# A graph kernel on one core: the first key's walk begins two steps later beside the second key's scatters

## The reference

```python
ex1 = e * x[src]
ex2 = e * x[dst]
mi = jnp.zeros_like(x).at[dst].add(ex1)
mo = jnp.zeros_like(x).at[src].add(ex2)
h = jnp.concatenate([mi, mo, x], axis=1)
h = jnp.tanh(h @ W1 + b1)
h = jnp.tanh(h @ W2 + b2)
h = jnp.tanh(h @ W3 + b3)
return jnp.tanh(h @ W4 + b4)
```

```python
edge_index = jnp.stack([src, dst])
x = _layernorm(x + _L0_gnn_ref(x, edge_weight1, edge_index, ...), axis=-1)
x = _layernorm(x + _L1_gnn_ref(x, edge_weight, edge_attr_3, edge_index, ...), axis=-1)
```

## Time and profile before

| | us |
|---|---|
| median of three runs | 2017.97 |
| lowest and highest | 2016.92, 2019.26 |
| the profiled execution | 2020.07 |
| its span in the profile | 2018.3 |
| last scatter of the second key begins | 1073.55 |

### The profile page before, as it was taken

One profiled execution on the slowest core, in us unless ns is written; L12 is line 12 of the kernel. 1 busy time (PEld: TensorE's weight loads), 2 busy tenths in 40 slices (PEclk: granted clock), 3 DMA queues, 4 the chain that ended last, 5 costly groups with the idle time before them and its releaser, 6 DMA issues. The chain is left out here.

```text
span 2018.3 us, 22733 instructions
## 1 busy us (share of the span) xinstructions
PE 1246.5 (62%) x5510; PEld 865.2 (43%) x5510; DVE 1086.3 (54%) x3123; ACT 627.4 (31%) x1638; POOL 1254.0 (62%) x1315
## 2 busy tenths in 40 slices
PE   5733444222226754433314689999589999998663
PEld 1311122111114543333203556666357777777553
DVE  9844544333313334544313647777547777776576
ACT  0100000000002210000006956666344444442785
POOL 6477777777757777777773113333488877871244
PEclk8766665666669986665557989999779999999676
DMA  1011111111137864544215535455313333332586
GB/s 34 21 34 33 31 31 34 34 34 34 34 102 213 216 189 131 149 130 136 81 40 134 151 103 155 151 160 154 103 37 79 99 100 84 94 100 79 147 214 167
DMA packets 330291, 204.52 MB, mean 101 GB/s; under 512 B 32299, under 2 KB 318704, under 8 KB 330160
## 3 DMA queue, kind: packets, MB, share of 16 engines
q1 hardware_dynamic: 269008, 140.38, 26.2%
q0 software_dynamic: 35280, 49.84, 8.7%
q10 hardware_dynamic: 25872, 12.85, 2.2%
HBM read 124.03 MB, written 78.92 MB: 101 GB/s over the span
## 5 line engine op out<-in xcount | busy, mean ns | idle before, releaser
L472 POOL DMA_INDIRECT placed<-pay,pos_i x392 | 396.3, 1011 | 155.0 <-issue 135.0
L467 POOL DMA_INDIRECT gat<-in_x,key_i x392 | 395.1, 1008 | 126.8 <-issue 116.3
L1018 DVE TENSOR_TENSOR pay<-bank,wj 128x512 f32<-128x512 f32 x98 | 67.5, 689 | 446.4 <-PE bank L785 432.2
L780 PE MATMUL bank<-ident,gat 128*128 128x128 f32 x98 | 38.8, 396 | 409.8 <-DMA gat<-in_x,key_i 398.3
L514 POOL DMA_INDIRECT gat<-x_d,src_i x196 | 253.2, 1292 | 59.0 <-issue 52.0
L1100 DVE TENSOR_TENSOR res<-res,bank 128x128 f32 x588 | 168.5, 286 | 146.1 <-PE bank L827 34.2
L897 PE MATMUL bank<-prod,ident 128*128 128x280 f32 x896 | 218.3, 402 | 0.0
L827 PE MATMUL bank<-woh,pw 128*128 128x128 f32 x784 | 143.4, 349 | 110.5 <-ACT woh L629 59.2
L780 PEld LDWEIGHTS bank<-ident,gat 128*128 128x128 f32 x98 | 17.6, 180 | 431.4 <-DMA gat<-in_x,key_i 414.4
L55 ACT ACTIVATE xt<-bank 128x128 f32<-128x128 f32 x98 | 26.8, 274 | 549.4 <-PE bank L780 549.3
L897 PEld LDWEIGHTS bank<-prod,ident 128*128 128x128 f32 x896 | 171.8, 192 | 47.0 <-issue 0.6
(11 more groups left out here) (155 smaller groups left out, 2325.9 us busy)
## 6 DMA issues: line engine op xcount, KB each, us to landing
pw<-placed SPq DMA_DIRECT2D x588, 68.0 KB, 2.1
pw<-placed SPq DMA_DIRECT2D x98, 272.0 KB
xin<-in_x_t SPq DMA_DIRECT2D x98, 256.0 KB, 3.1
hot_d<-woh SPq DMA_DIRECT2D x49, 256.0 KB, 2.4
x_d<-res POOLq DMA_DIRECT2D x49, 256.0 KB, 3.8
oh<-hot_d SPq DMA_DIRECT2D x28, 448.0 KB, 4.2
placed<-pay SPq DMA_DIRECT2D x28, 448.0 KB, 5.5
out<-out ACTq DMA_DIRECT2D x49, 256.0 KB, 2.7
```

Of the source, the lines that this page charges most:

```text
L467: pool.indirect_dma_start(gat[:, t, :], None, x, bass.IndirectOffsetOnAxis(ap=key_i[:, 1 - c, t:t + 1], axis=0)).then_inc(s_gat[n // CHUNK ...
L472: pool.indirect_dma_start(placed[c].rearrange("t p r -> (t p) r"), bass.IndirectOffsetOnAxis(ap=pos_i[:, c, t:t + 1], axis=0), pay[i % 4][ ...
```

## The change

The first walk gets a start step: batches 0 to 2 belong to step 2 and not to step 0, and so on, and its last batch to step 18 instead of 16. The second walk begins at step 19 instead of 17, and its last group is in step 43 instead of 41. Nothing is added or taken away.

```diff
-        FIRSTS, LAST_FIRST, EXTRAS = 3, 17, 2
+        FIRSTS, FIRST_FROM, LAST_FIRST, EXTRAS = 3, 2, 19, 2
...
-            return range(min(FIRSTS * q, NG), min(FIRSTS * (q + 1), NG))
+            return range(min(FIRSTS * max(q - FIRST_FROM, 0), NG), min(FIRSTS * max(q + 1 - FIRST_FROM, 0), NG))
```

## The result

| | before | changed |
|---|---|---|
| median, us | 2017.45 (4 runs) | 2003.48 (4 runs) |
| lowest and highest | 2016.83, 2019.26 | 2000.88, 2004.72 |
| span of the profiled execution | 2018.3 | 2002.8 |

The ratio is 0.9928, 95% interval 0.991 to 0.9945: the change makes the kernel faster, by 14.0 us between the medians, 0.55% to 0.9%. The forecast was 2003.0.

What follows compares the result with a forecast made beforehand. POOL's row of DMAs was taken to bound the second key's stage. The profiled 2020.07 us less 15.0 is 2005.1; being 2.1 above the median, the median goes from 2017.97 to about 2003.0, range 2001.0 to 2006.0.

Steps and rivals of the forecast that it cites:

- POOL bounds the stage, and what follows hangs on its last scatter: Second key's steps: each microsecond taken from POOL's row of DMAs moves everything behind it by a microsecond.
- The long wait is for a payload behind three batches: Ahead of group 49's first scatter: POOL loses 14.99 us to a payload whose projection stands behind three walk batches.
- Two steps suffice, with 5.7 us of slack: Change of key: group 51's payload is ready at 597.62, wanted at 603.3; one step would leave POOL starved.
- The overlap costs POOL about 0.1 us: From 582.6 to 597.6, walk loads beside POOL's DMAs: POOL loses 0.05 us on each of two groups.
- The walks' later end costs nothing: Second walk's end: two more loaded steps cost 9.4 us at most, within group 95's 10.3 us lead.
- Rival 1: Between groups 50 and 51: POOL starves if the first walk step grows over 5.7 us; 2010.6 if doubled; chance 5%.
- Rival 2: Change of key: DVE's one-hots in five newly overlapping batches hold POOL 4.4 us, giving 2007.4; chance 4%.
- Rival 3: Ahead of group 49: POOL waits for its queue or positions, not the payload; time stays 2018.0; chance 4%.
- Rival 4: Near the stage's end: the second walk's two steps come out there, 5.7 us slower, 2023.7; chance 2%.
- PE's clock: Behind the stage: 3.6 us at the lower clock, worth about 1.8 us, may fall out or come twice.

Runs made afterwards that it cites:

- experiment 1: Changed kernel with the walks begun one step later than before instead of two; 2007.07 us, ratio 0.9953 to the kernel before.
- experiment 3: Changed kernel with SP's first-walk loads also waiting until group 49's scatters have landed, one group later; 2009.73 us, ratio 0.9964 to the kernel before.
- experiment 10: Changed kernel with four batches of the first walk in a step instead of three; 2019.57 us, ratio 1.0015 to the kernel before.
- experiment 2: Changed kernel with the walks begun three steps later than before instead of two; 2003.58 us, ratio 0.9933 to the kernel before.
- experiment 9: Changed kernel with the second walk four more steps later (steps 23 to 47); 2001.60 us, ratio 0.9923 to the kernel before.
- experiment 11: Changed kernel with four more DVE compares behind each batch of the first walk; 2002.62 us, ratio 0.9922 to the kernel before.
- experiment 4: The changed kernel itself, unaltered, against the kernel before; 2000.90 us, ratio 0.992.
- experiment 8: The changed kernel once more, unaltered, against the kernel before; 2000.93 us, ratio 0.992.
- experiment 5: Changed kernel with the second walk four more steps later (steps 23 to 47), on the slower chip; 2147.01 us, ratio 1.0004 to the kernel before.
- experiment 7: Changed kernel with four more DVE compares behind each first-walk batch, on the slower chip; 2149.47 us, ratio 1.0014 to the kernel before.
- experiment 6: Changed kernel with four first-walk batches in a step instead of three, on the slower chip; 2157.95 us, ratio 1.0058 to the kernel before.

## Why the prediction was right, point by point

- **POOL bounds the stage, and what follows hangs on its last scatter.** Shown: the wait that went was 15.0 us, and in the four comparisons of the changed kernel with the kernel before the medians fell by 14.0, 16.8, 15.7 and 14.5 us. In the first pair of profiles the time behind the last scatter changed by only 0.5 us, but one pair can't show that closely: it is 940.7 to 946.8 us in the four profiles of the changed kernel. Experiments 1, 3 and 10 show the other sign: gaps of 5.9, 7.3 and 19.0 us cost 6.2, 8.8 and 18.6 us.
- **The long wait is for a payload behind three batches.** Shown by experiment 1, which moved it to the next group.
- **Two steps suffice, with 5.7 us of slack.** The size was a little off. Measured, the third payload was ready for POOL 5.0 us early (5.86 less the handover of 0.83). The walk's first step, from the first load to the projection behind it, took 597.47 - 583.61 = 13.9 us instead of 13.3 with POOL's DMAs beside it; I had allowed 2.1 us for that and it cost 0.6; the landing of `xin` in that stretch went from 2.7 us to 3.1, where I had taken 3.4. The next payload came 9.8 us later, and the lead grew to 23 us by group 67. By the prediction's 9.64 us a step it would have come to about 17 (16 steps of 0.7 behind 5.9): the direction was right and the pace was taken from the first step alone, where SP's loads give 9.0. That one step would leave POOL starved was in the prediction too, and experiment 1 has it: 5.9 us.
- **The overlap costs POOL about 0.1 us.** Groups 49 and 50 took (604.45 - 583.86) / 2 = 10.30 us each, less than the 10.33 that I took. Nothing was lost there.
- **The walks' later end costs nothing.** Shown by experiments 2 and 9. The thinnest lead near the end, that of group 95, is 10.3 us before and after, and 10.0 in experiment 9.
- **Rival 1** (third payload late) did not happen, though experiment 3 shows that it was the nearest: its price beyond 5.0 us is one for one, and a single late load in the next step added 1.8 us. On the chip of the slower kind it did come about (last section). **Rivals 2, 3 and 4** are refuted by experiments 11, 1 and 9, on the other chips.
- **The range.** That the forecast came within 0.5 us is in part luck: the gains of the four comparisons lie 2.8 us apart, and the medians of experiments 4 and 8, 2000.90 and 2000.93, are just below the 2001.0 at which the range ends, beside kernels before of 2017.66 and 2016.64. Two parts move between executions of the same kernel: the start of the stage (the second key's first scatter lay at 583.86, 581.27, 579.26 and 580.95 in four profiles of the changed kernel) and the time behind its last scatter (944.3, 940.7, 945.1 and 946.8). The range had a term for PE's clock in the second; how much of it is the clock was not worked out.

## What to carry to other kernels

When an engine sits idle with "issue" as its releaser and nothing else is busy, look at the program order of the engines that feed it: here a wait for the producer's own last transfer had been written ahead of the next piece of work for it. Put as many pieces of that work ahead of the wait as cover its length, and count them: from group 49's first scatter it took 15.6 us until the payload behind the walk's first step was ready for POOL (598.59 + 0.83 - 583.86), and each piece covers 10.3. So one was too few (5.9 us left in experiment 1), two gave 5.0 us of slack, and a third bought nothing that could be measured. Then check that the steps behind it are shorter than the bound's pace, by whatever paces them (here three loads of 3.0 us each), or the slack is eaten and the stall comes back in small pieces, as with four batches.

## What the runs showed of the hardware that was not expected

One chip took 2146.39 us for the kernel before, 6% more than the others, in 23 runs within 2140.66 to 2150.98. The time lies in the scatter stage: in the profile of experiment 5 the last scatter begins at 1197.46 and the span is 2139.1, so 941.6 us follow it, about as many as the 944.3 above. In the profile of the same kernel on the other chip, that of experiment 9, the last scatter begins at 1057.06, 140.4 us earlier. POOL's DMAs take the same (0.96 to 1.00 us), but its gaps beyond the usual 0.30 add up to 137.7 us more, 54.3 of them with the first key. In the first walk of the second key it waits 2.8 to 3.0 us ahead of each of the groups 52 to 65. The timeline of one step there:

```profile
712.05 0.39 PE L785 MATMUL bank<-wsl,xt 128*128 128x128 f32 x2
712.15 1.00 POOL L472 DMA_INDIRECT placed<-pay,pos_i  x1 [0.30 <-issue]
...
715.69 0.28 ACT L55 ACTIVATE xt<-bank 128x128 f32<-128x128 f32 x1 [11.75 <-remote]
715.73 0.69 DVE L1018 TENSOR_TENSOR pay<-bank,wj 128x512 f32<-128x512 f32 x1 [9.67 <-remote]
715.86 0.20 ACT L55 ACTIVATE pay<-kqs 128x4 f32<-128x4 f32 x1
...
717.23 1.04 POOL L472 DMA_INDIRECT placed<-pay,pos_i  x1 [2.81 <-issue]
```

PE's projection ends at 712.44 and the payload, which needs nothing else, starts 3.3 us later, and ACT's copy of the turned rows at the same moment; on the other chips the payload follows the start of the projection by 0.43 us (597.47 to 597.90 above). Something delays ACT and DVE here, and the profile calls it "remote". It isn't only these two: ahead of 637.69 in the same trace PE has waited 25.08 us for "remote". The clock differs as well: the mean granted clock of the execution is 0.737 in the profile of experiment 5 and 0.775 in that of experiment 9, and PE's matmuls of L817 take 851 ns on average against 654. Whether that is a cause or comes of PE's waiting, and what "remote" is, stays open. The step then takes 715.73 - 702.85 = 12.9 us against POOL's 10.3, so POOL waits in each step of the first walk, and a gap filled at the change of key would likely be given back. That was not tried: the changed kernel did not come to run on that chip. Its nearest relative there, experiment 5, was level with the kernel before (1.0004, 0.9989 to 1.0018), where the same kernel in experiment 9 has 0.9923.

On that chip rival 1 of the prediction came about. The rows at the change of key in the profile of experiment 7:

```profile
631.20 0.40 SPq L372 DMA_DIRECT2D xin<-in_x_t  x1
632.35 11.84 SPq L317 DMA_DIRECT2D pw<-placed  x4
645.58 0.70 SPq L372 DMA_DIRECT2D xin<-in_x_t  x1
...
666.36 0.39 PE L785 MATMUL bank<-wsl,xt 128*128 128x128 f32 x2
...
668.28 1.04 POOL L472 DMA_INDIRECT placed<-pay,pos_i  x1 [16.57 <-issue]
```

SP's second load stands 14.4 us behind its first, where it is 3.1 in the changed kernel (583.61 and 586.74), and the walk's first step takes 666.36 - 631.20 = 35.2 us instead of 13.9. So the third payload is late in spite of two payloads ahead, and group 51 waits 16.57 us; it waits 18.23 in the profile of experiment 6 and 3.94 in that of 5. The same kernels have no such gap ahead of group 51 in experiments 9 to 11. The slack of 5.0 us is a figure of the other chips.
